# Weighing in three unequal column chunks per two key tiles, with the row maxima taken over 1024, 512 and 512 columns

## What is computed

```python
q = (xn @ Wq.T + bq).reshape(b, s, 16, 16) * SCALE
k = (xn @ Wk.T + bk).reshape(b, s, 16, 16)
v = (xn @ Wv.T + bv).reshape(b, s, 16, 16)
scores = einsum('bqhd,bkhd->bhqk', q, k)
probs = softmax(scores, axis=-1)
out = einsum('bhqk,bkhd->bqhd', probs, v) @ Wo.T + bo
```

## Time and profile before

| | |
|---|---|
| median of 3 runs | 3329.87 us (3329.33 to 3333.35) |
| span of the profiled execution | 3325.6 us |
| PE busy | 3272.2 us (98%) |
| PEld busy | 1696.8 us (51%) |
| DVE busy | 2868.3 us (86%) |
| ACT busy | 2516.8 us (76%) |
| POOL busy | 947.6 us (28%) |
| granted TensorE clock, mean | 0.997 of 2.4 GHz |

### The profile page before, as it was taken

How to read it: one execution, slowest core, us unless ns; L and a number is a source line. 1 busy time by engine, 2 the same in 40 slices (tenths; PEclk the granted TensorE clock), 3 DMA queues, 4 the chain that set the end, 5 groups by cost and what they waited for, 6 DMA issues and landing times. The chain is left out here.

```text
span 3325.6 us, 68210 instructions
## 1 busy us (share of the span) xinstructions
PE 3272.2 (98%) x20848; PEld 1696.8 (51%) x20848; DVE 2868.3 (86%) x3022; ACT 2516.8 (76%) x5655; POOL 947.6 (28%) x1403
## 2 busy tenths in 40 slices
PE   7999999999999999999999999999999999899999
PEld 6444444444444444444444444444444444488887
DVE  7758999999999999999999999999999999566666
ACT  3558888888888888888888888888888888644443
POOL 2550222222222222222222222222222222344444
PEclk9999999999999999999999999999999999999999
DMA  6783333333333333333333333333333332355554
GB/s 201 204 237 52 58 57 57 57 56 58 55 55 60 58 57 56 57 57 57 55 55 55 55 55 55 55 55 55 55 55 55 55 55 62 110 161 160 166 160 123
DMA packets 139843, 271.64 MB, mean 82 GB/s; under 512 B 30144, under 2 KB 75264, under 8 KB 127296
## 3 DMA queue, kind: packets, MB, share of 16 engines
q1 hardware_dynamic: 137472, 266.71, 37.7%
q10 hardware_dynamic: 2112, 1.35, 0.1%
HBM read 173.59 MB, written 84.93 MB: 78 GB/s over the span
## 5 line engine op out<-in xcount | busy, mean ns | idle before, releaser
L959 DVE TENSOR_REDUCE half_max<-m_ps 128x1 f32<-128x1024 f32 x2006 | 2366.8, 1220 | 193.4 <-PE m_ps L886 188.8
L853 ACT ACTIVATE prob<-s_ps 128x512 f32<-128x512 f32 (+1 forms) x5120 | 2187.4, 522 | 404.4 <-PE s_ps L896 398.5
L896 PE MATMUL s_ps<-q_feat,k_feat 50*128 50x512 f32 (+1 forms) x5120 | 1535.0, 396 | 4.9 <-ACTq L843 2.1
L886 PE MATMUL m_ps<-k_feat,q_feat 48*128 48x512 f32 x4012 | 1358.3, 443 | 7.4
L896 PEld LDWEIGHTS s_ps<-q_feat,k_feat 50*128 50x128 f32 x5120 | 798.7, 184 | 977.4 <-ACT prob L853 869.1
L905 PE MATMUL a_ps<-prob,v_head 128*32 128x512 f32 x8192 | 1091.5, 605 | 0.0
L886 PEld LDWEIGHTS m_ps<-k_feat,q_feat 48*128 48x128 f32 x4012 | 594.9, 185 | 215.6 <-DVE half_max L959 214.1
L905 PEld LDWEIGHTS a_ps<-prob,v_head 128*32 128x32 f32 x8192 | 161.3, 108 | 249.2 <-issue 230.4
L695 POOL CAST shift<-row_max 128x16 fp32r<-128x16 f32 x63 | 12.3, 195 | 945.0 <-DVE row_max L961 945.0
L688 POOL COPY v_head<-v_all 128x256 f32 (+1 forms) x64 | 25.3, 397 | 826.1 <-PE a_ps L905 826.0
L1233 ACT ACTIVATE g_hi<-g 128x512 fp32r<-128x512 f32 x128 | 81.0, 633 | 212.5 <-DVE g L1266 172.1
(11 more groups left out here) (146 smaller groups left out, 2001.7 us busy)
## 6 DMA issues: line engine op xcount, KB each, us to landing
q_feat<-q_parts SPq DMA_DIRECT2D x384, 128.0 KB, 4.2
k_feat<-k_parts SPq DMA_DIRECT2D x384, 128.0 KB, 5.6
q_parts<-parts SPq DMA_DIRECT2D x32, 512.0 KB, 4.5
k_parts<-parts SPq DMA_DIRECT2D x32, 512.0 KB, 4.6
att_dram<-att SPq DMA_DIRECT2D x64, 256.0 KB, 6.4
mask_bc<-mask_b SPq DMA_DIRECT2D x128, 128.0 KB, 4.4
x_in<-in_x SPq DMA_DIRECT2D x16, 512.0 KB, 4.1
xn_dram<-xn SPq DMA_DIRECT2D x16, 512.0 KB, 4.8
```

What stands on the lines that cost most here:

```text
L853: act.activation(prob[tile(r, kt) % R][:, cols(j)], s_ps[slot(r, kt, j) % R][:, wide(j)], ACT.Exp).then_inc(exped, 1)
L886: ins = pe.matmul(m_ps[p % 2][:, k * BLK:(k + 1) * BLK], q_feat[r % 2][LOW, qt * P:(qt + 1) * P], k_feat[r % 2][LOW, key:key + BLK], start ...
L896: pe.matmul(s_ps[slot(r, kt, j) % R][:, wide(j)], k_feat[r % 2][UP, kt * P:(kt + 1) * P], q_feat[r % 2][UP, cols(j)], start=True, stop=Tru ...
L959: dve.tensor_reduce(half_max[r][:, p // 2, p % 2:p % 2 + 1], m_ps[p % 2][:, :], AX.X, ALU.max).then_inc(maxed, 1)
```

## The change

It touches `attend` and the first passes that `project` runs ahead. Four things differ:

1. **Scores.** Five pieces for a key tile become four of 512 columns (`CUTS`, `wide` and `LAG` are gone; `NP` is 4).
2. **Maxima.** DVE takes three reductions for a query tile instead of two: one over the 1024 columns of `m_ps0`, then one over each 512-column half of `m_ps1` (`MAX_BANKS`, `max_source`). Each matmul of the first pass raises `piece` itself, and a half of `m_ps1` can be written again as soon as it alone has been reduced. PE waits on `maxed` three times for a query tile, not twice.
3. **Weighing.** Two key tiles a and b = a + 1 are handled as one step. In it PE weighs columns 160 to 512 of each group for tile a - 3, all 512 columns for tile a - 2, and columns 0 to 160 for tile b - 2 (its rest follows in the next step). These are three groups of weighing matmuls for two tiles, not two.
4. **Order.** The matmuls of the first pass stand singly between score pieces. `EARLY` = 5 query tiles, which are the same 10 pairs. The transposition on DVE comes after the first reduction of query tile 2 and not before pair 5, and `collect` comes after piece 3 of tile 1.

```diff
-    CUTS = (0, BLK, 2 * BLK, 3 * BLK, 3 * BLK + BLK // 2, S)
-    NP = len(CUTS) - 1
+    TURN_AT = 2
+    NP = QB
+    CUT = 160
...
-                pe.wait_ge(exped, slot(g, kt, NP - 1) + 1 + R)
+            def weigh(g, r, kt, lo=0, hi=BLK):
+                if lo == 0:
+                    if kt == 0:
+                        pe.wait_ge(v_ready, g + 1)
+                        pe.wait_ge(att_read, g + 1)
+                    pe.wait_ge(exped, slot(g, kt, NP - 1) + 1 + R)
                 for qb in range(QB):
...
+                    ins = pe.matmul(a_ps[qb * VW:(qb + 1) * VW, lo:hi], v_head[r % R][:, kt, :],
+                                    prob[tile(r, kt) % R][:, qb * BLK + lo:qb * BLK + hi],
...
-                for kt in range(ST):
-                    a, b = half(kt, 0), half(kt, 1)
-                    score(g, it, r, kt, 0)
-                    a(0)
-                    a(1)
-                    score(g, it, r, kt, 1)
-                    score(g, it, r, kt, 2)
-                    if kt >= LAG:
-                        weigh(g, r, kt - LAG)
...
-                    score(g, it, r, kt, 3)
-                    b(0)
-                    score(g, it, r, kt, 4)
-                    b(1)
+                for kt in range(0, ST, 2):
+                    m = 4 * kt
+                    weigh_behind(kt - 3, CUT, BLK)
+                    for j in range(3):
+                        score(g, it, r, kt, j)
+                        shift_key(m + j)
+                    weigh_behind(kt - 2)
+                    score(g, it, r, kt, 3)
+                    for j in range(3, 6):
+                        shift_key(m + j)
+                    score(g, it, r, kt + 1, 0)
+                    score(g, it, r, kt + 1, 1)
+                    weigh_behind(kt - 1, 0, CUT)
+                    score(g, it, r, kt + 1, 2)
+                    shift_key(m + 6)
+                    shift_key(m + 7)
+                    score(g, it, r, kt + 1, 3)
...
             def maxima(n, r, turn_at=TURN_AT, lo=0):
...
+                    for o, banks in enumerate(MAX_BANKS):
+                        if (qt, o) == (turn_at, 1):
+                            turn_shift(n - 1)
+                        last_key += banks
+                        dve.wait_ge(piece, n * PIECES + qt * 4 + last_key)
...
+                        dve.tensor_reduce(half_max[r][:, qt, o:o + 1], max_source(m_ps, o), AX.X, ALU.max).then_inc(maxed, 1)
```

More of the change, by code:

```diff
@@ L164, in build @@
             k_feat = [sb(f"k_feat{r}", [P, S], F32R, ctx=first) for r in range(2)]
-            half_max = [sb(f"half_max{r}", [P, ST, 2], ctx=first) for r in range(HEAD_RING)]
+            half_max = [sb(f"half_max{r}", [P, ST, 3], ctx=first) for r in range(HEAD_RING)]
             row_max = [sb(f"row_max{r}", [P, ST], ctx=first) for r in range(HEAD_RING)]
@@ L442, in first_pass @@
             def first_pass(n, p):
-                if p == 0:
-                    pe.wait_ge(fed_low[n], 16 * LOADS)
-                pe.wait_ge(maxed, n * PAIRS + p + 1)
                 qt, half = divmod(p, 2)
                 for k in range(2):
-                    key = half * 2 * BLK + k * BLK
-                    ins = pe.matmul(m_ps[p % 2][:, k * BLK:(k + 1) * BLK], q_feat[n][low, qt * P:(qt + 1) * P],
-                                    k_feat[n][low, key:key + BLK], start=True, stop=True)
-                ins.then_inc(piece, 1)
+                    j = half * 2 + k
+                    if p == 0 and k == 0:
+                        pe.wait_ge(fed_low[n], 16 * LOADS)
+                    if j != 1:
+                        pe.wait_ge(maxed, n * OPS + max_op(qt, j) + 1)
+                    pe.matmul(m_ps[half][:, k * BLK:(k + 1) * BLK], q_feat[n][low, qt * P:(qt + 1) * P],
+                              k_feat[n][low, j * BLK:(j + 1) * BLK], start=True, stop=True).then_inc(piece, 1)
             with pe.Fori(0, BEFORE) as blk:
@@ L788, in _ @@
                 sp.wait_ge(done, 16 * NBLK + 16)
-            sp.wait_ge(piece, PAIRS)
+            sp.wait_ge(piece, PIECES)
             feed(2, 0, LOWER, fed_low)
@@ L864, in step @@
                         exp(g, r, kt, j, first)
-                        if not first and (kt, j) == (LAG - 1, 2):
+                        if not first and (kt, j) == (1, NP - 1):
                             collect(g - 1)
@@ L940, in _ @@
                 step(g, 0, g, following=g + 1 < HEADS, after=g + 2 < HEADS)
-            for kt in range(ST - LAG, ST):
-                weigh(HEADS - 1, HEADS - 1, kt)
+            weigh(HEADS - 1, HEADS - 1, ST - 3, CUT, BLK)
+            weigh(HEADS - 1, HEADS - 1, ST - 2)
+            weigh(HEADS - 1, HEADS - 1, ST - 1)
         @block.vector
```

109 lines of the change are left out of this document (53 added, 56 removed).

## The result

| | before | after |
|---|---|---|
| median | 3331.26 us (4 runs, 3329.33 to 3333.35) | 3171.28 us (4 runs, 3165.62 to 3178.08) |
| span of the profiled execution | 3325.6 us | 3170.1 us |
| a head, between two joinings of the maxima | 41.04 us | 38.46 us |

The ratio is 0.9522, interval 0.9508 to 0.9535: 4.8% faster. The forecast was 3150 us with a range of 3125 to 3215. The time lies in the range and 21 us over the forecast.

What follows compares the result with a forecast made beforehand. A PE-ACT loop was taken to bound the kernel, with DVE just under it. At 38.2 us a head, 63 heads save 2.84 each, 179 us: 3325.6 - 179 + 4.3 = 3151, stated as 3150 us, range 3125 to 3215.

Steps and rivals of the forecast that it cites:

- The bound of before: In attend, a loop of waits between PE and ACT, 2.55 us a tile, with DVE just under it at 2.28.
- A short reduction starts 0.604 after the one before it: On DVE, 512-column reductions start 0.604 us apart, so a query tile costs DVE 2.35 us, not 2.28.
- Rival B: On DVE, the short reduction is dearer, 0.64 us or more between starts: 3215 to 3300 us, chance 0.08.
- DVE's floor of 38.09 a head: DVE's least time for a head: sixteen tiles of 2.35 us plus 0.49 at the border.
- Prices of the weighing groups, 0.99, 0.73 and 0.41: On PE, microseconds for weighing 512, 352 and 160 columns: four cycles a column plus 0.14 a group.
- Rival A: PE's switches between weighing and passes cost more in short groups: 3175 to 3235 us, chance 0.15.
- The loop of 4.73 for two tiles: PE and ACT's way round in the changed order takes 4.73 us for two tiles, against 5.10 before.
- The two loops together, 38.2: DVE's floor of 38.09 us plus half of today's border cost, 0.12, gives 38.2 us a head, 2.84 less.
- The third group is covered: The third weighing group's 0.35 us on PE lies under PE's idling for ACT; uncovered it costs 2.8 us a head.
- Rival C: Reads and writes of m_ps1 exclude each other: 3628 us; chance 0.05, shared with any other new wait making it slower.
- Rival D: No change, 3330 us: the saved piece only moves the wait, in a loop that was missed; chance 0.04.
- Outside the loop: In project, three reductions add at most 1.4 us, 0 taken; no new stall on a DMA at head borders.

Runs made afterwards that it cites:

- e6: Kernel before with only the maxima in three reductions per query tile, scores, weighing and order as before: 3335.91 us, ratio 1.0019 to before.
- e5: Changed kernel with ACT's wait for the odd tile's weighing one piece earlier and the cut at 224 columns instead of 160: 3113.95 us, ratio 0.9348 to before.
- e12: Changed kernel with the first score of tile b one place earlier on PE, behind two first-pass matmuls instead of three: 3135.24 us, ratio 0.9410 to before.
- e1: Changed kernel with ACT's wait for the weighing of the odd tile taken one exponential earlier, before the even tile's last piece: 3141.96 us, ratio 0.9436 to before.
- e4: Changed kernel with each reduction of m_ps1 reading only 256 of its 512 columns, leaving out part of the maximum: 3171.40 us, ratio 0.9519 to before.
- e2: Changed kernel with the weighing cut at 224 columns instead of 160, so groups of 288 and 224: 3138.87 us, ratio 0.9419 to before.
- e3: Changed kernel with two full weighing groups for two tiles, the third group left out: 3304.97 us, ratio 0.9922 to before.
- e8: Changed kernel without the three maxima, with two 1024-column reductions per query tile as before: 3550.77 us, ratio 1.0660 to before.
- e10: Changed kernel with ACT's wait for the odd tile's weighing one piece earlier and the cut at 256 columns: 3117.38 us, ratio 0.9348 to before.
- e7: Kernel before with four score pieces of 512 columns instead of five, everything else as before: 3373.87 us, ratio 1.0129 to before.

## Why the prediction was right, and what it missed

- **The bound of before**, a loop between PE and ACT with DVE just under it: right. e6 relieves nothing and adds to DVE, and the head stays at 41.0.
- **A short reduction starts 0.604 after the one before it:** measured 0.60, with a duration of 0.679. Rival B is out. The Trainium skill, Perfetto Trace Analysis, section Optimizing Scalar/DVE Operations, has some 125 ns for each DVE operation on PSUM; the trace of after doesn't agree, since 0.60 between starts leaves 0.06 over 0.54 for 512 columns.
- **DVE's floor of 38.09 a head:** too high by 0.45. A tile needs 2.33, not 2.35. At the border the joining adds 0.24 (1511.17 - 1510.46 + 0.12 - 0.60 in rounded starts, and 0.835 - 0.598 as medians of the single records; forecast 0.23), but the transposition only 0.12 (1517.20 - 1517.08), where I had taken 0.26 over from the earlier trace rows. There DVE hadn't gone on at once behind the transposition: the next reduction started 0.27 later with no idle time named, and I booked that as its price. The floor is 16 x 2.33 + 0.36 = 37.64, and e5 reaches 37.60.
- **Prices of the weighing groups, 0.99, 0.73 and 0.41:** measured 1.00, 0.72 and 0.41, and 0.52 and 0.62 for 224 and 288 columns. Rival A is out. The switch in and out of a weighing costs the same however short the group.
- **The loop of 4.73 for two tiles:** measured 4.79. This is the step that failed. The term was "the second starts 1.11 - 0.62 = 0.49 later": I let ACT alone set that distance and took for granted that the score of b was there. The changed order puts three first-pass matmuls ahead of that score, so its semaphore comes just when ACT could take it (0.48 after the start of the exponential before), and behind two waits the exponential starts 0.57 after its predecessor. The 0.08 are cut to 0.06 by hundredths in the other terms. e12 (score one place earlier) took it away and e1 (wait moved) most of it, for 36 and 29 us.
- **The two loops together, 38.2:** measured 38.46 on average. I had DVE as the binding one and half a border on top. In fact PE and ACT bind (e4: no effect of 19% less busy time in DVE's reductions; e1, e2 and e12: 29 to 36 us from edits on the other loop). That the number came out near is in part luck: both floors lie within 1 us of each other, and of my two terms the one was too high and the other too low. Two signs that I had named came true all the same: DVE was busy for 2315 of the 2340 us from 260 to 2600, and its wait for PE fell to near nothing. Neither tells a bound from an engine just under it.
- **The third group is covered:** right. e3 without it loses 2.1 us a head.
- **Rival C**, reads and writes of `m_ps1` that exclude each other: out. DVE waits for PE 5 us in 2200, and e6, which has these reads and writes in the old order, keeps its head of 41.0. **Rival D:** out by the result; e8 shows, though, that a new order which outruns DVE's releases would have been slower than before.
- **Outside the loop:** the first joining comes 2.3 us later than before (230.16 against 227.89), where I had allowed up to 1.4 and taken 0. One execution can't decide that: in e1, e2, e5, e10 and e12, whose edits lie all in attend, the same joining comes at 228.6 to 232.1. No score load waits for a DMA at a border in 400 to 2600 us, as forecast.
- **A sum in the ranges:** a reduction at 0.61 would by the forecast's own terms add 63 x 16 x 2 x 0.006 = 12 us, so 3162 and not 3157.

The sum by these steps: I forecast 63 x 2.84 = 179 us off the profiled execution, and 155.5 came off (3325.6 - 3170.1). Over the 62 heads between the joinings the difference of 38.46 - 38.2 = 0.26 makes 16, the standstill 5.7, and the start, the last head and the end together under 2. The median lies 1.2 us above the span here and not 4.3, so 3325.6 - 155.5 + 1.2 = 3171.3 stands where the forecast had 3325.6 - 179 + 4.3 = 3151.

## What to carry to other kernels

When two engines hand pieces to each other, write down for every piece in the loop when its data comes and when its engine could take it, with all that stands ahead of it in the other engine's queue: one matmul in the wrong place cost 36 us here. A long group that both sides wait for can be cut so that a part of it lies under the other engine's work: without that cut 25 of the 160 us were left (e3), and with the wait moved and the cut at 224 instead of 160 it brought another 57 us, until the second floor was met. Full busy time and an idle time of nothing in the list of waits don't make an engine the bound: take work away from it and see whether the time moves.

## What the hardware showed that I had not expected

- An exponential with two waits costs nothing more while its semaphores come early (0.49 between starts in e7 and e12). Where the semaphore of its score comes last, 0.48 after the start of the exponential before, it starts 0.57 after that one with two waits (after) and 0.51 with one (e1, median of 442): 0.06 us for the second wait.
- A score's semaphore can wait for the matmul ahead of it in the queue, although the two run beside each other on different rows: it comes 0.05 us after the modelled end of the first-pass matmul ahead, in all 429 tiles of after.
- PE can stand still for 2 to 3.8 us with no semaphore named that it waits for (in ten kernels of the eleven), 2.8 to 4.4 us after its program leaves a loop. In after the granted clock is then 0.50 for 6.8 us, in which a score piece takes 0.79 us and not 0.50, and the head loses 5.7 us; in e1, e5 and e10, with 2.0 to 2.3 us from matmul to matmul, the clock stays full and the head loses about 2. It survives a shift of the code by 128 instructions.
- A fp32 weighing in four column groups of the array takes what four cycles a column and 0.14 us give, from 160 to 512 columns (0.41, 0.52, 0.62, 0.72, 1.00).
